# A block's counting product and its followers, one step later

## The reference

```python
x = L0_attn_x
x = x + 0.5 * ffn(layernorm(x))
x = x + attention(layernorm(x))
x = x + 0.5 * ffn(layernorm(x))

# in ffn, x is (tokens, 256); 16 experts, 4 per token, inner width 128
logits = jnp.einsum('th,eh->te', x, gate_w)
probs = jax.nn.softmax(logits, axis=-1)
topk_w, topk_idx = jax.lax.top_k(probs, TOP_K)
topk_w = topk_w / jnp.sum(topk_w, axis=-1, keepdims=True)
scores = jnp.einsum('tk,tke->te', topk_w, one_hot)
act = jax.nn.silu(jnp.einsum('th,ehi->tei', x, w1)) * jnp.einsum('th,ehi->tei', x, w3)
expert_out = jnp.einsum('tei,eih->teh', act, w2)
out = jnp.einsum('teh,te->th', expert_out, scores)
```

## The kernel before

| engine | order in unit e |
|---|---|
| PE | front(first, 0), up 0, front(first, 1), up 1, front(second, 0), down half 0 of e - 1, front(second, 1), down half 1 of e - 1 |
| DVE | gate of e, add half 0 of e - 1, front(first), add half 1 of e - 1, front(second) |
| ACT | silu of e, front pieces, cut of the weights of group e + 2 (L546) |

## Time and profile before

### The profile page before, as it was taken

The page is one execution under the profiler, slowest core; times in us unless marked ns, Lnnn a source line. Parts: engine busy times, 40 slices in busy tenths (PEclk is TensorE's granted clock), DMA queues, the critical chain, the costliest instruction groups (busy, mean ns, idle before and its releaser), DMA issues. The chain is left out here.

```text
span 1564.6 us, 32677 instructions
## 1 busy us (share of the span) xinstructions
PE 1416.8 (91%) x9796; PEld 964.5 (62%) x9796; DVE 1033.0 (66%) x2636; ACT 775.6 (50%) x1317; POOL 640.7 (41%) x679
## 2 busy tenths in 40 slices
PE   4899999999978869999999899999698999999997
PEld 3687888888856623343333333333276878888886
DVE  5575646366788678887788688786267564445567
ACT  4312566555135424665566466567451245655530
POOL 3361443767645460232222122223235406176765
PEclk9899999999989957999999899999789999999999
DMA  7651566888326910443335253300131227588873
GB/s 256 223 201 57 179 199 193 263 249 249 99 74 163 237 66 1 65 61 43 43 43 67 34 67 43 42 3 2 41 107 63 94 71 230 159 254 248 261 235 109
DMA packets 159221, 199.08 MB, mean 127 GB/s; under 512 B 18180, under 2 KB 132440, under 8 KB 159064
## 3 DMA queue, kind: packets, MB, share of 16 engines
q1 hardware_dynamic: 140632, 146.67, 36.0%
q0 software_dynamic: 18432, 50.36, 10.1%
HBM read 105.21 MB, written 91.49 MB: 126 GB/s over the span
## 5 line engine op out<-in xcount | busy, mean ns | idle before, releaser
L1636 ACT ACTIVATE attn_prob<-attn_b_ps 128x1024 f32<-128x1024 f32 (+3 forms) x352 | 303.8, 870 | 214.9 <-PE attn_b_ps L1838 213.8
L505 POOL DMA_INDIRECT xs_dram<-ffn_xn,ffn_index x192 | 188.4, 981 | 228.8 <-DVE ffn_index L780 172.5
L1818 PE MATMUL attn_a_ps<-k_rows,q_rows 96*128 96x512 bf16 (+3 forms) x768 | 252.3, 352 | 24.5 <-DVEq L1674 7.5
L519 POOL DMA_INDIRECT ffn_gathered<-ys_dram,ffn_index x192 | 196.6, 1024 | 86.8 <-issue 56.1
L1687 DVE TENSOR_REDUCE attn_max_a<-attn_a_ps 128x1 f32<-128x512 f32 (+2 forms) x304 | 202.6, 688 | 43.3 <-PE attn_a_ps L1818 24.1
L1573 POOL TENSOR_SCALAR_AFFINE_SELECT attn_prob<-attn_prob 128x512 f32<-128x512 f32 x128 | 81.1, 634 | 359.2 <-ACT attn_prob L1636 356.6
L824 DVE TENSOR_TENSOR ffn_xs_lo<-ffn_xt_ps,ffn_xs_hi 128x512 fp32r<-128x512 f32 x144 | 97.7, 678 | 154.8 <-ACT ffn_xs_hi L596 154.3
L1818 PEld LDWEIGHTS attn_a_ps<-k_rows,q_rows 96*128 96x128 bf16 x768 | 75.3, 99 | 189.9 <-DVE attn_max_a L1687 79.9
L1862 PE MATMUL attn_o_ps<-attn_prob,attn_v_now 128*17 128x256 f32 (+1 forms) x2560 | 189.0, 368 | 0.0
L1838 PE MATMUL attn_b_ps<-q_rows,k_rows 98*128 98x512 bf16 (+3 forms) x768 | 187.9, 333 | 0.3 <-ACT attn_prob L1636 0.3
L1684 DVE CUSTOM_DVE_ANT_0 attn_scored<-attn_a_ps,mask_wide 128x512 bf16<-128x512 f32 (+1 forms) x256 | 155.1, 623 | 40.2 <-PE attn_a_ps L1818 35.3
(11 more groups left out here) (209 smaller groups left out, 2732.2 us busy)
## 6 DMA issues: line engine op xcount, KB each, us to landing
ffn_xs<-xs_dram SPq DMA_DIRECT2D x138, 256.0 KB, 3.5
ys_dram<-ffn_y SPq DMA_DIRECT2D x138, 256.0 KB, 2.9
xs_dram<-ffn_y SPq DMA_DIRECT2D x16, 768.0 KB, 11.2
qk_parts<-proj_cut SPq DMA_DIRECT2D x32, 384.0 KB, 3.0
k_rows<-qk_parts SPq DMA_DIRECT2D x96, 128.0 KB, 4.7
q_rows<-qk_parts SPq DMA_DIRECT2D x96, 128.0 KB, 7.4
ffn_w_stage<-in_L_ffn_w_dram SPq DMA_DIRECT2D x64, 128.0 KB, 2.5
x_res<-in_L_attn_x_dram SPq DMA_DIRECT2D x4, 1024.0 KB, 8.7
```

Source lines behind the costliest of these rows:

```text
L505: pool.indirect_dma_start(xs_dram[(b + 1) % 2], bass.IndirectOffsetOnAxis(index[:, b, i, k:k + 1], 0), xn[:, b % 2, i, :], None, bounds_ch ...
L519: pool.indirect_dma_start(gathered[:, t % G_RING, k, :], None, ys_dram[b], bass.IndirectOffsetOnAxis(index[:, b, i, k:k + 1], 0), bounds_c ...
L1636: act.activation(prob[PROB[kt]][:, h:h + heads, prob_at(kt, kt * P):prob_at(kt, S)], b_ps[:, slot, :].rearrange("p (h t) -> p h t", h=head ...
L1818: ins = pe.matmul(a_ps[:, bank, i * keys:end], q_rows[q][0:SROWS, h0 + i, qt * P:(qt + 1) * P], k_rows[q][0:SROWS, h0 + i, first:first + k ...
```

## The change

`count_before` moves from offset 11 to offset 12, and `count`, `place_rows`, `place_experts` and `place_scores` from 12 to 15 to 13 to 16. `OFFSETS` grows to 17 so that the last part has a place. Nothing is added or removed: the same instructions run, in another order on PE and DVE. ACT, POOL and SP have the same streams as before.

```diff
-OFFSETS = 16
+OFFSETS = 17
...
             parts = {0: early_stats, 1: late_stats, 3: inverse_root, 8: router, 9: compare, 10: choose, 11: weigh,
-                     12: count, 13: place_rows, 14: place_experts, 15: place_scores}
+                     13: count, 14: place_rows, 15: place_experts, 16: place_scores}
...
-                if o == 11 and late:
+                if o == 12 and late:
                     count_before(b)
```

## The result

The changed kernel takes 1555.61 us (median of 20 runs, 1551.11 to 1565.48) against 1563.03 us of the kernel before, timed beside it (20 runs). The ratio is 0.9965, with a 95% interval of 0.9952 to 0.9978: 5.5 us faster, 3.4 to 7.5. One run of the kernel before took 2251 us and is not in the ratio. The forecast time of 1555.2 us was met. The gain of 8.6 us from which it was made lies above that interval.

A forecast was written before the change was run, and what follows sets the result against it. PE, busy 91% of the span, was taken as the bound, its largest wait being 17.4 us for `chosen`. Heads 4.8 plus routed stage 3.8 made 8.6 us off 1563.8: 1555.2 us, range 1550.5 to 1560.8.

The forecast's parts named there:

- The wait in the head: Block 1, both `ffn`: 2.35 us of PE work moves ahead; the wait for `chosen` shrinks from 6.0 to about 3.7 us.
- The clock behind it: Behind both heads' waits: low-clock stretches stay 6.1 and 3.3 us, term zero; bounds 4.6 us won or 1.4 us lost.
- DVE behind it: Both heads: DVE's set starts earlier, then PE waits some 1.2 us for its add; 2.1 and 2.7 us won, together 4.8.
- bounds 3.3 to 9.1: Range for both heads' gain in us: 3.3 with the long low-clock stretch, 9.1 with no low clock.
- Waits in the routed stage: Blocks 2 and 3: waits of 1.21 us for `chosen` become 0.25 for `xs_lo`; 0.95 us won four times, 3.8 us.
- The lower bound of the term, 0: Routed stage, blocks 2 and 3: no gain, if DVE stays late through its next parts.
- the waits only move: Rival: routed waits for `chosen` become full waits for `xs_lo`, only heads gain 3.3 to 4.8 us; 1559.0 to 1560.5, chance 0.17.
- The late index: Scatters of blocks 2 and 3 come some 3 us later, block 1's index at about the old time; all hidden.

The follow-up runs named there:

- e2: Changed kernel with only blocks 2 and 3 at the later offsets, block 1 at the old ones; ratio to the kernel before 1.0006.
- e4: Changed kernel with ACT's cuts of the last two weight groups, and POOL's `w_lo` with them, one dense unit later; ratio to the kernel before 0.9983.
- e6: Changed kernel with the four parts behind the counting product spread to offsets 13, 14, 16 and 18; 1553.27 us in one run.
- e7: Changed kernel with the last two weight cuts in units 9 and 10 instead of 4 and 5, ahead of POOL's scatter; 1578.86 us.
- e9: e8 with the last two weight cuts in units 9 and 10 on ACT and inside POOL's scatter; 1554.82 us, ratio to the kernel before 0.9949.
- e5: Changed kernel with the routed stage's expert numbers loaded into PE's registers without bounds; 1708.17 us, ratio to the kernel before 1.0932.
- e11: Changed kernel with the next step's two register loads ahead of the up product instead of behind it; 1580.34 us in one run.
- e8: Kernel before with block 1's counting product and the parts behind it two offsets later, blocks 2 and 3 unchanged; 1548.72 us, ratio 0.9926.
- e10: e9 with the four parts behind the counting product at offsets 14, 15, 17 and 19; 1552.49 us, ratio to the kernel before 0.9937.
- e12: e10 with POOL taking block 2's root behind tile 6 of the scatter instead of tile 7; 1546.89 us, ratio to the kernel before 0.9894.

## Why the prediction was right, and where it was wrong

1. *The wait in the head.* Right in place and size: 3.75 us twice, where 3.7 was said, and `chosen` not made sooner.

2. *The clock behind it.* Right that it falls, wrong in what was assumed of its length: low stretches of 3.4 and 3.1 us, not 6.1 and 3.3. The length is no property of the wait: the equal waits of e2, 5.99 us, left 2.8 and 3.4 us at 1.2 GHz behind them, and the waits of e4, 4.20 us, left 5.7 and 3.0. So the 6.1 us of the earlier trace rows belonged to that one execution, and the 3.2 us won in the first head, where 2.1 were said, owe about 1 us to the luck of the executions that were profiled. Against e2, whose first head has the old order and a short low stretch, the first dense stage won 2.2 us (107.7 less 0.85 us that e2 is longer ahead of the wait, 106.9, against 104.7). This agrees with the free-running period that the prediction cited from the Trainium skill (TensorE: Matmul & The Clock Gate, "Part 1: The HAM clock gate"): a wait doesn't fix how much of the low stretch follows it.

3. *DVE behind it.* The wait of L981 for `x_res` came as said (1.2 us said, 1.23 and 1.22 seen), and e6 shows its cause. The two times that made it were both missed alike: DVE's set ended at 85.31 + 0.88 = 86.19 and not at 87.8, for with the shorter low stretch DVE idled 0.25 us in it and not 2.0, and PE was there at 86.24 - 1.23 = 85.01 and not at 86.7. The prediction let `w_lo` fall on `weigh` at no cost while the clock is low, and it gave 1.8 us per head as the price at full clock, by the Trainium skill's rule on the shared port pair (SBUF — State Buffer, "SBUF: two separate sides"). The 2.24 us of one small product beside a `w_lo` of 2.38 agree with that rule. The price was not paid: the delay of up to 71.04 - 69.85, about 1.2 us, was gone in the first head by the gate of unit 6, where DVE waited for PE, and e7 has the same 1.22 us of wait with `weigh` free and the clock high. Heads: 4.8 said, 5.8 seen, of which about 1.0 is the long low stretch of the one execution before; bounds 3.3 to 9.1.

4. *Waits in the routed stage.* This is the step that failed. 3.8 us were said; e2 shows none (1.0006). The prediction let PE reach the up product with `xs_lo` at 165.2, and this came true: it started 0.22 us behind `xs_lo`, with no wait. What was left out is what PE's instruction stream has to do behind it: two register loads. In the kernel before the stream had come to them as the array began the product, so that they lay under it; held for `xs_lo` until the array was there too, it came to them 0.8 us after, and 0.70 us of idle time came to light. From the end of `xs_lo` to the transposes that begin the next step it took 168.86 - 165.16 = 3.70 us before and 165.18 - 161.37 = 3.81 after. The chain from `choose` through `xs_lo` and the stream was as long as the one through the counting product, and removing one of two equal chains wins nothing. The lower bound of the term, 0, held, but by another cause than the one named with it. The rival "the waits only move" was right of this stage, with the stream in the place of `xs_lo`; its gain of 3.3 to 4.8 us, from the heads alone, lies at the lower end of the measured interval.

5. *The late index.* Hidden, as said: PE's wait for the rows behind the root is 1.71 us before and after. Block 1's index came 2.2 us sooner, where "about the old time" was said (POOL's scatter began at 79.90, before at 82.09), and the spare time at the root fell from 2.43 to 0.26 us (116.91 in the trace after), about what 2.43 - 2.1 of the prediction leaves. How thin this cover is, e9 shows: with 5 us more on POOL ahead of the root the wait became 3.62 us.

So the heads alone make up the measured 5.5 us (3.4 to 7.5): 5.8 in the profiled executions, some 4.8 without the long low stretch, and nothing at the four places of the routed stage. The time itself was met within half a microsecond by luck: the routed 3.8 us were too much, and the median of the changed kernel lies 7.4 us below that of the kernel before, in the upper part of the interval. The profiled executions differ by 11.2 us. What goes beyond the heads lies ahead of the first wait (0.7), between the two `ffn` and in the attention (2.8 together with the first tail), and in the second routed stage (240.2 us before, 237.7 after), while the first is 0.5 us longer (238.4 and 238.9). A whole routed stage varies by as much in kernels that have the same order in it (238.6 us the second of e2, 242.3 that of e7), so I give the change none of this.

## What to carry to other kernels

Before a wait is counted as won, follow the consumer's own instruction stream through the same stretch: register loads and address arithmetic that lay under the wait, or under the product behind it, come to light when it goes. A step that is moved later pays where the waiting engine has work ready that depends on none of the late data, and only as much as that work is long; then look at what was hidden behind it next (here DVE's dense set, then POOL's order of cuts, scatter and root). And let one engine's long instruction not start just ahead of another's short critical one when the two were seen to exclude each other: moving it by a unit moved the loss from the scans to `chosen`.

## What the runs showed of the hardware that was not expected

- A register loaded without bounds costs an assertion at every use in PE's stream: most routed steps 4.2 to 4.7 us instead of 3.0 to 3.3, the kernel 146 us slower than the one before (e5).
- The same pair of register loads costs little behind the up product (in the kernel before L1020 waits 4.9 us for issue in 12 times), and 25 us over the kernel ahead of it (e11): PE's stream runs only just ahead of the array in these steps.
- One small DVE product beside POOL's `w_lo` takes 2.24 to 2.46 us instead of 0.28. It was seen for two products whose inputs both lie in SBUF, `chosen` in e4 and the one of `weigh` in the changed kernel, which start 0.03 and 0.3 us behind it. The scans, with inputs in SBUF too, were held by one of the eight alone, which took 1.94 us in the changed kernel where the others took 0.22. The gates and adds, which read one input from PSUM, took their usual 0.69 us and 0.88 us for two beside a `w_lo` (in the kernel before at 74.84 and 75.54, under the one from 74.26 to 76.63).
- Behind waits of 3.75 to 6.01 us the clock stood at 1.2 GHz for 2.8 to 6.1 us, and the length of the wait did not set it (6.1 and 3.3 us before, 2.8 and 3.4 in e2, 5.7 and 3.0 in e4, 3.4 and 3.1 after). One wait of 1.52 us was followed by such a stretch in one head and not in the other (e8), waits of 2.04 and 2.06 us in neither (e7), and without a wait the clock stayed at 2.4 GHz there (e9, e10, e12).
